# Scores of a banded attention: merged and shifted in PSUM by VectorE instead of copied out by ScalarE

## The reference

```python
xp  = jnp.pad(x, ((0, 0), (k - 1, 0), (0, 0)))          # k = 32
q   = (x @ Wq.T).reshape(b, t, h, e) / scale            # h = 8 heads, e = 32
kk  = (xp @ Wk.T).reshape(b, tp, h, e) / scale
v   = (xp @ Wv.T).reshape(b, tp, h, e)
idx = jnp.arange(t)[:, None] + jnp.arange(k)[None, :]
dot = jnp.einsum('bthe,btkhe->bthk', q, kk[:, idx])
attn = jax.nn.softmax(dot, axis=-1)
out = jnp.einsum('bthk,btkhe->bthe', attn, v[:, idx])
return out.reshape(b, t, h * e) @ Wu.T + bu
```

## Time and profile before

| | |
|---|---|
| median of 3 runs | 625.59 us |
| profiled execution, its own time | 628.51 us |
| its span, first to last instruction | 626.9 us |
| mean granted TensorE clock | 0.829 of 2.4 GHz |
| busy: TensorE / VectorE / ScalarE / GpSimd | 418.2 / 478.1 / 204.1 / 350.9 us |
| banded attention's units, first score matmul to last output matmul | 369.8 to 462.9 us |

### The profile page before, as it was taken

How to read it: one execution, slowest core, us unless ns; L and a number is a source line. 1 busy time by engine, 2 the same in 40 slices (tenths; PEclk the granted TensorE clock), 3 DMA queues, 4 the chain that set the end, 5 groups by cost and what they waited for, 6 DMA issues and landing times.

```text
span 626.9 us, 8773 instructions
## 1 busy us (share of the span) xinstructions
PE 418.2 (67%) x3280; PEld 209.7 (33%) x3290; DVE 478.1 (76%) x622; ACT 204.1 (33%) x227; POOL 350.9 (56%) x307
## 2 busy tenths in 40 slices
PE   6678864676676667667767879687163997554660
PEld 2453323222222223222223335575132435441220
DVE  1998998799999999999996317999416556996332
ACT  2564883223233232323230544221010126112220
POOL 6667004579999999998996321789980000430000
PEclk8986887769999999999999998655566996578775
DMA  8540023935554574555430000000000000000000
GB/s 282 171 136 9 2 85 96 209 82 155 152 149 137 148 181 134 142 161 155 149 105 1 8 6 1 2 2 1 2 22 1 2 0 1 2 3 8 3 5 33
DMA packets 29523, 46.11 MB, mean 74 GB/s; under 512 B 18146, under 2 KB 19588, under 8 KB 28452
## 3 DMA queue, kind: packets, MB, share of 16 engines
q1 hardware_dynamic: 27044, 45.12, 26.0%
q0 software_dynamic: 2368, 0.37, 0.5%
q10 hardware_dynamic: 64, 0.00, 0.0%
HBM read 43.57 MB, written 1.11 MB: 71 GB/s over the span
## 4 chain that ended last, share of the span: by engine, by line
DVE 31%; POOL 30%; PE 19%; issue 12%; ACT 3%; DMA 2%; DVEq 1%; SPq 0%; ACTq 0%; POOLq 0%
POOL dBu L882 14%; POOL hit L867 7%; PE ps L1983 3%; POOL work L959 3%; POOL work L961 3%; DVE hC L1525 2%; PE ps L2193 2%; PE ps L2305 2%; POOL work L948 2%; DVE hst L1504 2%; DVE hC L1295 2%; DVE hC L1291 1%; DVE work L1751 1%; PE ps L2458 1%; PE ps L2220 1%
## 5 line engine op out<-in xcount | busy, mean ns | idle before, releaser
L2121 PE MATMUL ps<-hC,ident 128*128 128x512 f32 x256 | 123.1, 603 | 0.0
L1143 ACT ACTIVATE ps<-work,a_neg 128x1020 f32<-128x1020 f32 x64 | 71.2, 1115 | 155.7 <-DVE hst L1504 102.7
L1504 DVE TENSOR_TENSOR_SCAN hst<-ps,dBu 128x1024 f32<-128x1024 f32 x43 | 98.3, 2287 | 5.1 <-POOL dBu L882 3.8
L2105 PE MATMUL ps<-late,pick_state 96*128 96x512 bf16 x128 | 40.4, 399 | 69.2 <-DVE hC L1525 67.9
L867 POOL DMA_INDIRECT hit<-in_L_attn_edge_values,tab_i x64 | 67.0, 1047 | 29.6 <-DMA hit<-in_L_attn_edge_values,tab_i 20.4
L882 POOL TENSOR_TENSOR dBu<-work,dA 128x1024 f32<-128x1024 f32 x32 | 75.3, 2360 | 7.1 <-DMA dA<-b_rows_all 4.3
L2121 PEld LDWEIGHTS ps<-hC,ident 128*128 128x128 f32 x256 | 49.8, 195 | 43.8 <-issue 35.4
L882 POOL TENSOR_TENSOR dBu<-work,b_sb 128x1024 f32<-128x1024 f32 x16 | 39.8, 2488 | 38.8 <-DVE work L1488 37.3
L1525 DVE TENSOR_TENSOR hC<-hst,ps 128x1024 f32<-128x1024 f32 x43 | 51.5, 1198 | 1.8 <-PE ps L2105 1.1
L1504 DVE TENSOR_TENSOR_SCAN work<-ps,dBu 128x1024 f32<-128x1024 f32 x21 | 48.0, 2287 | 2.0 <-POOL dBu L882 1.3
L2105 PEld LDWEIGHTS ps<-late,pick_state 96*128 96x128 bf16 x128 | 7.9, 99 | 120.9 <-DVE hC L1525 116.9
(11 more groups left out here) (369 smaller groups left out, 833.4 us busy)
## 6 DMA issues: line engine op xcount, KB each, us to landing
dA<-b_rows_all SPq DMA_DIRECT2D x64, 256.0 KB
b_sb<-b_rows_all SPq DMA_DIRECT2D x32, 256.0 KB
work<-b_rows_all SPq DMA_DIRECT2D x32, 256.0 KB
work<-in_L_attn_edge_index SPq DMA_DIRECT2D x6, 1024.0 KB, 7.2
dA<-in_L_attn_edge_index SPq DMA_DIRECT2D x1, 1024.0 KB, 5.3
dBu<-in_L_attn_edge_index SPq DMA_DIRECT2D x1, 1024.0 KB, 8.4
hit<-in_L_attn_edge_values,tab_i POOLq DMA_INDIRECT x64
late<-work SPq DMA_DIRECT2D x12, 64.0 KB, 2.0
```

Of the source, the lines that this page charges most:

```text
L1143: nc.scalar.activation(dst[:, :, 1:], src[:, :, 1:], ACT.Exp, scale=a_neg[:, n:n + 1]).then_inc(dA_sb, 1)
L1504: V.tensor_tensor_scan(h_buf[i % 3], dA_ps[k], dBu[:, k, :], 0.0, ALU.mult, ALU.add).then_inc(scan_done, 1)
L2105: last = T.matmul(bank(2 + h), pick_state[:, n, :, :].rearrange("p v i -> p (v i)"), parts[:, j * NT + h * HALF:j * NT + (h + 1) * HALF], ...
L2121: last = T.matmul(bank(6 + h), ident[:, :], hC[:, i % 2, h * HALF:(h + 1) * HALF], start=False, stop=(n == S - 1))
```

## The change

The copy by ScalarE is left out. The merge is done in place, in PSUM: VectorE copies the older half over the own-window half where the mask is set. Maximum and subtract read that half in PSUM, and the subtract is the first to write the SBUF buffer. So the subtract, instead of the merge, is now the last reader of banks 0 to 3, and the scores of the next unit wait for it (`s2_shifted`). The wait for a free buffer (`p2_t`) goes from ScalarE's copy to VectorE's subtract.

```diff
-            def window_keys(u):
-
-                act.wait_ge(s2_ps, u + 1)
-                if u >= 3:
-                    act.wait_ge(p2_t, u - 2)
-                nc.scalar.activation(s2_buf[u % 3].rearrange("p (s k) -> p s k", k=C),
-                                     bank(0, 4).rearrange("p (s w k) -> p s w k", w=2, k=C)[:, :, 1, :],
-                                     ACT.Copy).then_inc(s2_copied, 1)
-
...
-            window_keys(0)
...
-                if u < UNITS - 1:
-                    window_keys(u + 1)
...
+            scores2 = bank(0, 4).rearrange("p (s w k) -> p s w k", w=2, k=C)
+
             def window_merge(u):
-                seg = s2_buf[u % 3].rearrange("p (s k) -> p s k", k=C)
-                dve.wait_ge(s2_copied, u + 1)
-                V.copy_predicated(seg, older.bitcast(I32).unsqueeze(1).to_broadcast([P, SEGS, C]),
-                                  bank(0, 4).rearrange("p (s w k) -> p s w k", w=2, k=C)[:, :, 0, :]
-                                  ).then_inc(s2_read, 1)
+                dve.wait_ge(s2_ps, u + 1)
+                V.copy_predicated(scores2[:, :, 1, :], older.bitcast(I32).unsqueeze(1).to_broadcast([P, SEGS, C]),
+                                  scores2[:, :, 0, :]).then_inc(s2_merged, 1)
 
             def window_shift(u):
                 seg = s2_buf[u % 3].rearrange("p (s k) -> p s k", k=C)
-                dve.wait_ge(s2_read, u + 1)
-                link(V.tensor_reduce(mx2[:, u % 2, :], seg, AX_X, ALU.max))
-                V.tensor_tensor(seg, seg, mx2[:, u % 2, :].unsqueeze(2).to_broadcast([P, SEGS, C]),
+                dve.wait_ge(s2_merged, u + 1)
+                link(V.tensor_reduce(mx2[:, u % 2, :], scores2[:, :, 1, :], AX_X, ALU.max))
+                if u >= 3:
+                    dve.wait_ge(p2_t, u - 2)
+                V.tensor_tensor(seg, scores2[:, :, 1, :], mx2[:, u % 2, :].unsqueeze(2).to_broadcast([P, SEGS, C]),
                                 ALU.subtract).then_inc(s2_shifted, 1)
...
                 if u == 0:
                     pe.wait_ge(qm_sb, 4)
                 else:
-                    pe.wait_ge(s2_read, u)
+                    pe.wait_ge(s2_shifted, u)
```

More of the change, by code:

```diff
@@ L403, in hybrid_kernel @@
         w2_sb = sem("w2_sb")
-        s2_copied = sem("s2_copied")
         qm_ps = sem("qm_ps")
@@ L408, in hybrid_kernel @@
         v2_ps = sem("v2_ps")
-        s2_read = sem("s2_read")
+        s2_merged = sem("s2_merged")
         v2_sb = sem("v2_sb")
```

## The result

The changed kernel took 631.27 us (median of 4 runs, 630.13 to 634.55) beside 625.99 us for the kernel before (median of 4, 624.32 to 626.54) in the same comparison: a ratio of 1.0097, 95% interval [1.0052, 1.0142]. It is slower by 5.3 us; the forecast was 631.0 us. Two later comparisons gave 1.0065 [1.0038, 1.0092] and 1.0082 [1.0047, 1.0118], so 4 to 5 us. Medians are of all runs; ratios leave out the few runs that are over 1.5% above the fastest of their kernel.

The account below looks back on a forecast made before the run. GpSimd's chain was taken to bound the steady part, with VectorE hardly slacker. Four units at +5.5 us and the head at -0.15 made +5.3 us on the 625.59 us median: 631.0 us, range 625.5 to 635.

Parts of the forecast that it names:

- the step that decides: Last hunk: scores of unit u+1 wait for unit u's subtract instead of its merge, freeing the banks some 3.1 us later.
- The loop: Steady units: subtract to next subtract through scores, outputs, values, transposes and maximum closes a chain that sets the cadence.
- Its size: Steady units at half clock: 10.60 us per unit, four units 42.4 us against 36.85, +5.5 us.
- Subtract from PSUM 1.22 us, not stretched; gathers 1.0: From unit 3 on, subtract unstretched, giving VectorE 0.84 us or more per unit and the gather 0.8 us.
- The merge in PSUM: VectorE's in-place merge: 1.3 us taken, 1.20 to 2.29 possible; covered in the steady part, up to +2 us in first four units.
- The head: Up to unit 3's subtract: gains of copy and stretching used up by the later release, -0.15 us.
- my bounds: Range for the stretch up to unit 3's subtract: -1.3 us (release costs nothing) to +2 us.
- The tail: From unit 6's scaling to the stage's end: 22.4 us of GpSimd work stays untouched, so the delay arrives whole.
- The clock: TensorE's granted clock stays 0.50 (1.2 GHz) from about 395 us to the end of the stage.
- the prediction's faster rival: TensorE at 2.4 GHz from unit 3 on: cadence 7.6 us, four units 30.4 us, total 618 us; chance 0.12.
- The rival's limit: Full-clock case decides once scores, outputs and values together are under 4.3 us, against 7.4 at half clock.
- The sum: Whole kernel: 5.5 - 0.15 = +5.3 us, 633.8 us in a like profile, 631.0 us for the median.

Follow-up runs that it names:

- late_release: Kernel before with only the scores' wait moved from the merge to the subtract; copy and SBUF merge stay: 632.89 us, 1.0093.
- release_exp: Changed kernel with the next unit's scores waiting for ScalarE's exponential, behind the subtract: 642.15 us, 1.0249.
- outputs_first: Changed kernel with the output matmuls of unit u-3 moved ahead of the scores' wait: 626.21 us, 1.0003.
- before_again: Kernel before, unedited, run again for a second trace: 626.11 us, 0.9989.
- after_third: Changed kernel, unedited, run a third time: 630.15 us, 1.0082.
- after_again: Changed kernel, unedited, run again for a second trace: 629.71 us, 1.0065.
- warm_before: Kernel before with eight matmuls of zeros per unit added in TensorE's order: 630.54 us, 1.0060.
- warm_after: Changed kernel with matmuls of zeros where TensorE would wait, four ahead of the scores, four behind the first values: 624.02 us, 0.9946.
- warm_early: Changed kernel with matmuls of zeros already from unit 2 and the output banks cleared one gap earlier: 626.14 us, 0.9990.
- warm_again: The program of warm_after, unchanged, run again: 628.83 us, 1.0002.
- merged_copy: Kernel before with the merge in PSUM ahead of ScalarE's copy, which releases the banks; maximum and subtract read SBUF: 627.79 us, 1.0016.
- outputs_first_warm: Changed kernel with outputs ahead of the scores' wait and matmuls of zeros added: 628.53 us, 1.0032.

## Why the prediction was right

The time was right (631.0 against 631.27), and so was the step that decides, the loop. That the time came within 0.3 us is luck, as the points on size, head and sum show. Point by point:

- **The loop**: shown. The scores wait for the subtract (below: releaser, us in total, times, longest, over the whole stage), the value transposes for TensorE, GpSimd for the reciprocal. late_release has it by one line, release_exp lengthens it by just what the release is later, outputs_first takes a part out of it, and the cadence falls by 1.0 us, to that of the next loop.

```profile
PE ps L2209 <- DVE work L1602: 6.4, 6, 1.7
...
DVE work L1623 <- PE ps L2221: 10.1, 8, 1.7
...
POOL work L947 <- DVE sm L1609: 25.9, 6, 13.2
```

- **Its size**: mis-sized. 9.85 us instead of 10.60, so four units cost +2.6 us and not +5.5. (The prediction's 8.94 us for a unit of VectorE before leaves out that two of the four take 9.49; its +5.5 was counted from the ends of the subtracts and isn't touched by that.) The terms: scores 3.62 instead of 4.22, outputs 1.76 instead of 1.96 (the longest row of the trace before; half of the eight are 1.83, and the next matmuls start 0.07 before such a record ends), the others within 0.05. I had taken 65.9 ns for a score matmul from the 3.82 us of the earlier trace rows, but in that order the scores run among the second value matmuls of the unit, and their record holds a part of these. Behind the new wait they run alone, 57.7 ns each (3.69 / 64). GpSimd waits at most 2.46 us in a unit of the steady part instead of "about 3" by the same error; the scores' own wait is 1.1 to 1.7 us from unit 3's scores on, because I forgot that TensorE finishes the second values of the unit in the meantime.
- **Subtract from PSUM 1.22 us, not stretched; gathers 1.0**: right in size (1225 ns over eight against 1888 before; 0.99). But late_release shows that at this cadence the SBUF subtract isn't stretched either. What I booked as a gain of the change was one of the slower cadence. The rows below are the changed kernel's groups of this stage (count, busy us, mean ns, idle before):

```profile
L1602 DVE TENSOR_TENSOR work<-ps,mx 128x1024 f32<-128x1024 f32 x8 | 9.8, 1225 | 0.3
...
L1593 DVE COPY_PREDICATED ps<-band,ps 128x1024 f32<-128x1024 int32 x8 | 9.8, 1226 | 13.5 <-PE ps L2209 13.5
...
L1599 DVE TENSOR_REDUCE mx<-ps 128x32 f32<-128x1024 f32 x8 | 9.5, 1186 | 0.0
```

- **The merge in PSUM**: 1226 ns, 0.07 below what I took. The maximum from PSUM is 1186 ns against 1179 from SBUF. The added fixed cost that the Trainium skill gives for a PSUM source ("VectorE: DVE Perf Modes", the section on the TRN2 errata), which I had put at 0.5 us over four units, is not in these rows.
- **The head**: mis-sized, -0.15 us predicted. I worked it out on the first trace of before, whose unit 3 ends its subtract at 32.2 us. The three changed executions have 30.0, 30.9 and 31.6: 2.2, 1.3 and 0.7 us earlier, the first outside my bounds. Against the second trace of before (29.6) they are 0.4 to 2.0 us later. What differs is where the clock falls for a short time. In the first trace of before it was 0.50 from 8.4 to 11.8 us behind the first score matmul, and unit 1's subtract ended at 15.9; in before_again it didn't fall there, and it ended at 13.8. All three traces of the changed kernel have 3.4 us at 0.50 in this part. In the first two they lie earlier (373.9 to 377.3 and 370.9 to 374.3), and unit 1's subtract ends at 14.2; in after_third they lie as in the first trace of before (376.8 to 380.2, 8.0 to 11.4 behind the first score), and it ends at 15.9. That pair is the one that compares like with like, and it gives -0.7. I had taken the place of the fall for a fixed property of the kernel. How often the kernel before has it, two traces can't say.
- **The tail**: right. From unit 7's subtract to the last output it is 23.9 us in both.
- **The clock**: right, 0.50 from 394.4 to the end of the stage in the changed kernel, with one short full stretch in after_again, where the last fall comes at 391.4 already. The rival's limit is 7.6 - 3.2 = 4.4 us, not 4.3. The Trainium skill's rule that continuous matmul work restores the full clock ("TensorE: Matmul & The Clock Gate", the table under "Why this matters for your kernels") was the prediction's faster rival. The unbroken 32.1 us at 0.50 in warm_before, behind which the clock did rise, disagree with it for this mix of matmuls.
- **The sum**: right by errors that lean against each other. I added the difference to the median of before, 625.59 us, but had worked it out against one execution of 628.51, in which the early fall of the clock made the head 2.6 us longer than in before_again. In the form in which it was derived, the forecast failed: "633.8 us in a profile like this one", with units 5.3 us longer. The three profiled executions took 630.13, 630.12 and 629.33 us, and their units are 0.3 to 1.9 us longer than in that trace. Set against before_again instead, the loop was 3 us too long and the head 0.5 to 2.1 us too short.

Against before_again the steady part (mean of three 39.2 against 36.8) and the head (30.8 against 29.6) make +3.6 us; the three comparisons measured 4.1 to 6.1 us by their ratios. So 0.5 to 2.5 us are **open**. By the like pair of above, after_third and the first trace of before, the two parts make only +1.9 us, and 2 to 4 us are open. The stretches ahead of the units and behind them vary by about 2 us between executions of one kernel (starts from 368.8 to 371.1, rests 164.0 to 165.8 for the changed one), with no edit in them, and the profiled executions are too few to average this out.

## What to carry to other kernels

When the last reader of a PSUM bank moves to a later instruction, write down everything that stands behind the next writer in its engine's order, and follow it back to that last reader: if it closes, and if its sum is longer than any other loop's and any engine's own work, it is the cadence at the clock of that stretch. The cure is then the order and not the operation; here moving one call ahead of the wait gave back all of the loss, until the next loop set the pace. Take a duration from a row in which the instructions run in the order that they will have, and look at two executions of the kernel before where the clock changes within the stretch.

## What the runs showed of the hardware

- **32 us of unbroken work passed before the clock came back.** TensorE was busy for 32.10 of 32.10 us at 1.2 GHz in warm_before; then the clock was full for 17 us. In warm_after the clock was back after 6.80 us, of which TensorE was busy for 6.47; in a second execution of the same program after 17.10 us, busy for 16.43. I can't predict from these rows when it returns.
- **A subtract with both large operands in SBUF** took 1.22 to 1.23 us away from GpSimd's products and 2.07 to 2.73 beside them, and the gather behind that product 1.79 instead of 0.99; with one operand in PSUM 1.23 throughout. That GpSimd's use of SBUF is the cause is what the rows suggest; no run took it away by itself.
- **A predicated copy within PSUM** took 1.20 to 1.23 us, from PSUM onto SBUF 1.29 to 1.31.
- **With matmuls added in one stage, a later one was longer; the cause is open.** In warm_after, warm_early, warm_again and warm_before the rest behind the units took 167.3 to 168.6 us instead of 163.9 to 165.8 in the two kernels and merged_copy (one profiled execution each). A part of it is a stall of TensorE in the graph attention, in which it waits for nothing that the profile shows (here warm_early's):

```profile
558.13 0.51 PE L2361 MATMUL ps<-work,hC 128*32 128x32 f32 x35 [1.86 <-issue]
```

In warm_after and warm_before the low clock behind the units also lasted some 20 us instead of 13 to 14. Against the added matmuls as the only cause: late_release, which has none, has a rest of 166.2 us, and outputs_first_warm, with more of them and a stall of 1.53 us at the same place, has 164.0.
